# Wide token repeats from a source read four times, and gate rows moved in one piece, in a convolution-attention and expert block

## The reference

```python
t = _to_tokens(x)                       # 4096 tokens per image, 32 features
xn = _ln_t(t)
router_probs = softmax(xn @ router_w + router_b)          # 8 experts
top_p, top_i = top_k(router_probs, 2)
top_p = top_p / sum(top_p)
expert_out = einsum('bnd,edc->bnec', xn, expert_w) + expert_b
t = t + einsum('bnk,bnkc->bnc', top_p, gathered)          # the two best experts, weighted
```

## Time and profile before

| | |
|---|---|
| median of 3 runs | 486.19 us (486.01 to 487.49) |
| profiled execution | 487.85 us, its span 486.2 us |
| busy: PE, DVE, ACT, POOL | 402.4, 390.1, 242.5, 104.6 us |
| DVE, tenths busy in 40 slices of 12.2 us | 0389578999999999999999875976897997997643 |
| DMA share, tenths, same slices | 8400000000000000000000001932164737727541 |
| SP's queue: token repeats, gate moves | 112 of 128 KB, 48 of 32 KB |
| POOL's queue: token repeats, stores | 16 of 128 KB, 16 of 256 KB |

### The profile page before, as it was taken

The page is one execution under the profiler, slowest core; times in us unless marked ns, Lnnn a source line. Parts: engine busy times, 40 slices in busy tenths (PEclk is TensorE's granted clock), DMA queues, the critical chain, the costliest instruction groups (busy, mean ns, idle before and its releaser), DMA issues.

```text
span 486.2 us, 12843 instructions
## 1 busy us (share of the span) xinstructions
PE 402.4 (83%) x4872; PEld 208.5 (43%) x4882; DVE 390.1 (80%) x511; ACT 242.5 (50%) x409; POOL 104.6 (22%) x152
## 2 busy tenths in 40 slices
PE   3786789999999999999999988469688698666863
PEld 1232346666666666666666543124234233111210
DVE  0389578999999999999999875976897997997643
ACT  3653367767777676677767670615323512102110
POOL 6730001011101110110111010003224324524632
PEclk9999779999999999999999998969899989879888
DMA  8400000000000000000000001932164737727541
GB/s 306 184 0 1 2 1 3 1 1 0 0 0 0 0 0 0 0 0 0 0 0 0 3 1 28 205 82 50 38 151 128 167 80 179 187 58 202 140 129 43
DMA packets 10901, 28.80 MB, mean 59 GB/s; under 512 B 3200, under 2 KB 4736, under 8 KB 10496
## 3 DMA queue, kind: packets, MB, share of 16 engines
q1 hardware_dynamic: 8400, 20.46, 16.6%
q0 software_dynamic: 2048, 6.29, 4.3%
q10 hardware_dynamic: 432, 1.77, 0.9%
HBM read 5.96 MB, written 4.19 MB: 21 GB/s over the span
## 4 chain that ended last, share of the span: by engine, by line
PE 45%; DVE 27%; issue 11%; ACT 6%; SPq 5%; DMA 2%; DVEq 1%; POOL 1%; POOLq 0%; ACTq 0%
PE psum L459 7%; DVE neg_max L927 6%; PE psum L321 5%; PE psum L476 5%; PE psum L341 4%; SPq L206 4%; PE psum L446 4%; PE psum L430 4%; DVE window_work L930 3%; PE psum L600 3%; PE psum L484 3%; PE psum L592 3%; PE psum L570 3%; DVE o_tok L938 2%; DVE rstd L363 2%
## 5 line engine op out<-in xcount | busy, mean ns | idle before, releaser
L728 ACT ACTIVATE probs<-psum 128x512 f32<-128x512 f32 x128 | 74.4, 594 | 25.1 <-PE psum L459 24.4
L930 DVE TENSOR_TENSOR window_work<-psum,neg_max 128x1024 f32<-128x1024 f32 x64 | 78.4, 1225 | 7.2
L927 DVE TENSOR_REDUCE neg_max<-psum 128x16 f32<-128x1024 f32 x64 | 77.0, 1203 | 7.3 <-PE psum L446 7.2
L459 PE MATMUL psum<-weights_sb,window_work 128*128 128x128 f32 x512 | 82.1, 283 | 0.9 <-ACT probs L728 0.9
L254 POOL TENSOR_TENSOR o_norm<-o_tok,o_rden 128x128 f32<-128x128 f32 x64 | 24.6, 406 | 249.8 <-DVE o_rden L940 249.8
L459 PEld LDWEIGHTS psum<-weights_sb,window_work 128*128 128x128 f32 x512 | 58.3, 142 | 43.5 <-issue 25.7
L476 PE MATMUL psum<-probs,v_cols 128*32 128x64 f32 x2048 | 55.4, 226 | 0.3 <-DVE o_tok L938 0.3
L592 PE MATMUL psum<-gate_rows,gate_sel_sb 128*128 128x512 bf16 (+1 forms) x118 | 42.3, 407 | 12.8 <-DVE window_work L1075 5.3
L1075 DVE TENSOR_TENSOR window_work<-stage,psum 128x512 f32<-128x512 f32 x48 | 31.8, 676 | 16.3 <-PE psum L592 10.9
L476 PEld LDWEIGHTS psum<-probs,v_cols 128*32 128x32 f32 x2048 | 34.6, 109 | 23.7 <-issue 20.6
L712 ACT ACTIVATE stage<-k_sb,weights_sb 128x512 f32<-128x512 f32 x64 | 44.3, 723 | 0.0
(11 more groups left out here) (95 smaller groups left out, 615.5 us busy)
## 6 DMA issues: line engine op xcount, KB each, us to landing
stage<-x_win SPq DMA_DIRECT2D x112, 128.0 KB, 2.6
out<-out_sb POOLq DMA_DIRECT2D x16, 256.0 KB, 2.5
stage<-in_x SPq DMA_DIRECT2D x3, 1024.0 KB, 14.4
stage<-x_win POOLq DMA_DIRECT2D x16, 128.0 KB, 3.7
gate_rows<-gate_parts SPq DMA_DIRECT2D x48, 32.0 KB, 1.8
stage<-in_x SPq DMA_DIRECT2D x2, 512.0 KB, 6.2
weights_sb<-weights ACTq DMA_DIRECT2D x1, 875.5 KB, 10.3
gate_f<-gate_sel ACTq DMA_DIRECT2D x1, 512.0 KB, 13.5
```

What stands on the lines that cost most here:

```text
L459: last = nc.tensor.transpose(bank[TURN_BANKS[v % 2]][:, b * P:b * P + P], heads.rearrange("p h k -> p (h k)"), const["c_ident"][:, :])
L728: nc.scalar.activation(probs[:, w % 4, :], bank[TURN_BANKS[w % 2]][:, :], ACT.Exp).then_inc(exp_done, 1)
L927: nc.vector.tensor_reduce(m_t, t, AX.X, ALU.max, negate=True).then_inc(max_done, 1)
L930: nc.vector.tensor_tensor(shifted_unit[:, unit % 2, :, :, :], t, m_t.unsqueeze(3).to_broadcast([P, IMG, HEADS, TOK]), ALU.add).then_inc(sh ...
```

## The change

- A token repeat becomes one DMA per image and pair. Its source names each of the 32 channel rows four times (a broadcast dimension behind the partitions), its destination is all 128 partitions of `x_rep`. Row (c, e) now lies in partition 4c + e, where it was 32e + c. All are issued by SP; POOL issues none. Each image has a semaphore of its own, and DVE waits for an image in front of the first unit that uses it.
- A gate move becomes one DMA per chunk: source 32 rows with their three parts, destination 96 rows of `gate_rows`, in the order (row, part). POOL's memset of `gate_rows` goes.
- The weights have to match the new row order. PE regroups the expert weights by a permutation matmul ahead of the attention, DVE builds the permutations (two copies) and copies the result to `experts_sb`. PE selects and reorders the 96 rows of `gate_sel` by two matmuls behind the router of quad 0 (`select_rows`), and ACT writes them as bf16; DVE's cast of `gate_sel` goes.

```diff
             def move_gates(ats):
                 for j, at in enumerate(ats):
-                    for s in range(SPLITS):
-                        sp.dma_start(gate_rows[32 * s:32 * s + 32, bass.ds(at, CHUNK)],
-                                     gate_parts[32 * j:32 * j + 32, s, :]).then_inc(gates_in[j], 16)
+                    sp.dma_start(gate_rows[:, bass.ds(at, CHUNK)],
+                                 gate_parts[32 * j:32 * j + 32, :, :]).then_inc(gates_in[j], 16)
             def repeat_tokens(at, pair):
-                for b in range(IMG if pair == 0 else IMG - POOL_IMAGES):
-                    for e in range(IMG):
-                        sp.dma_start(x_rep[32 * e:32 * e + 32, pair, b, :, :].rearrange("p j n -> p (j n)"),
-                                     t_norm[32 * b:32 * b + 32, bass.ds(at, 2 * CHUNK)]).then_inc(x_rep_in[pair], 16)
+                for b in range(IMG):
+                    sp.dma_start(x_rep[:, pair, b, :, :].rearrange("p j n -> p (j n)"),
+                                 t_norm[32 * b:32 * b + 32, bass.ds(at, 2 * CHUNK)].unsqueeze(1)
+                                 .to_broadcast([C, IMG, 2 * CHUNK])).then_inc(x_rep_in[pair][b], 16)
...
-            pool.memset(gate_rows[:, :], 0.0).then_inc(filled, 1)
...
-                        if j < POOL_IMAGES:
-                            repeat_tokens(i * 2 + u, IMG - 1 - j)
...
+            pe.wait_ge(regroup_ready, 2)
+            nc.tensor.matmul(bank[7][:, 2 * C:4 * C], regroup[:, 0:P],
+                             const["c_we"].rearrange("p a n -> p (a n)"), start=True, stop=True,
+                             skip_group_check=True).then_inc(bias_ps, 1)
...
+            def select_rows(pe):
+                pe.wait_ge(gate_in_loaded, 16)
+                pe.wait_ge(exp_done, CHUNKS * NW + EXP)
+                for u in range(2):
+                    last = nc.tensor.matmul(bank[6 + u][0:SPLITS * 32, :],
+                                            regroup[:, P:P + SPLITS * 32],
+                                            gate_in[:, u * CHUNK:u * CHUNK + CHUNK], start=True, stop=True)
+                last.then_inc(gate_sel_ps, 1)
...
             for j in range(QUAD):
                 router(0, j)
+            select_rows(pe)
             project(CHUNKS - 1, at=5)
...
             gate_logits(0)
+            act.wait_ge(gate_sel_ps, 1)
+            for u in range(2):
+                nc.scalar.activation(gate_sel[:, u * CHUNK:u * CHUNK + CHUNK]
+                                     .rearrange("p (k c e) -> p k e c", k=IMG, c=C),
+                                     bank[6 + u][0:SPLITS * 32, :].rearrange("p (k e c) -> p k e c", k=IMG, e=IMG),
+                                     ACT.Copy).then_inc(gate_sel_ready, 1)
             layer_norm(1)
...
             reciprocals_first(0)
+            dve.wait_ge(weights_loaded, 16)
+            nc.vector.tensor_copy(regroup[:, 0:P].rearrange("p (c e) -> p c e", e=IMG), ...)
+            nc.vector.tensor_copy(regroup[:, P:P + SPLITS * 32].rearrange("p (r s) -> p r s", s=SPLITS), ...)
...
             dve.wait_ge(bias_ps, 1)
+            nc.vector.tensor_copy(experts_sb[:, :, :].rearrange("p a n -> p (a n)"), bank[7][:, 2 * C:4 * C])
...
-            dve.wait_ge(gate_in_loaded, 16)
-            nc.vector.tensor_copy(gate_sel[:, :], gate_in)
...
-                    if j % 2 == 0:
-                        dve.wait_ge(x_rep_in[j // 2], quad * REPEATS[j // 2] + REPEATS[j // 2])
-                    if j == 2:
-                        dve.wait_ge(x_rep_pool, quad * (POOL_IMAGES * IMG * 16) + POOL_IMAGES * IMG * 16)
...
+                            if j % 2 == 0 and k < IMG:
+                                dve.wait_ge(x_rep_in[j // 2][k], quad * 16 + 16)
```

More of the change, by code:

```diff
@@ L89, in metaformer_block @@
         gate_parts = sb("gate_parts", [P, SPLITS, CHUNK], BF16)
-        gate_rows = sb("gate_rows", [P, QUADS * QUAD * CHUNK], BF16)
+        gate_rows = sb("gate_rows", [SPLITS * 32, QUADS * QUAD * CHUNK], BF16)
         logit, logit_t, g_a, g_b, g_mask1, g_mask2, g_rest, gate_t = (
@@ L107, in metaformer_block @@
         gate_in = gate_f32[:, 0:2 * IMG * P]
-        gate_sel = sb("gate_sel_sb", [P, 2 * IMG * P], BF16)
+        gate_sel = sb("gate_sel_sb", [SPLITS * 32, 2 * IMG * P], BF16)
+        experts_sb = sb("experts_sb", [P, 2, C])
+        regroup = sb("regroup", [P, P + SPLITS * 32])
         qb_scaled = sb("qb_scaled", [P, 1])
@@ L136, in metaformer_block @@
         biases_ready = sem("biases_ready")
+        regroup_ready = sem("regroup_ready")
+        gate_sel_ps = sem("gate_sel_ps")
+        gate_sel_ready = sem("gate_sel_ready")
         x_cur_ready = sem("x_cur_ready")
@@ L160, in metaformer_block @@
         gates_in = [sem(f"gates_in{j}") for j in range(QUAD)]
-        x_rep_in = [sem(f"x_rep_in{u}") for u in range(2)]
-        x_rep_pool = sem("x_rep_pool")
+        x_rep_in = [[sem(f"x_rep_in{u}{b}") for b in range(IMG)] for u in range(2)]
         gate_ps = sem("gate_ps")
@@ L175, in metaformer_block @@
         GATE_OPS = 26
-        POOL_IMAGES = 1
-        REPEATS = (IMG * IMG * 16, (IMG - POOL_IMAGES) * IMG * 16)
         DVE_UNITS = 2 * IMG - 2
@@ L212, in _ @@
             repeat_tokens(first[2], 1)
-            sp.wait_ge(filled, 4)
             sp.wait_ge(gate_step, GATE_OPS + ONE)
@@ L268, in scale @@
                 if j % 2 == 0 and i == 0:
-                    pool.wait_ge(x_rep_in[j // 2], quad * REPEATS[j // 2] + REPEATS[j // 2])
+                    pool.wait_ge(x_rep_in[j // 2][0], quad * 16 + 16)
                 pool.wait_ge(gate_copied, c * 2 + (i + 1))
@@ L285, in left @@
                 pool.sem_inc(out_free, 1)
[L287 to L293, removed]
             with pool.Fori(0, QUADS // 2) as i:
@@ L411, in _ @@
             nc.tensor.matmul(bank[7][:, 0:1], const["c_wp"][:, :], const["c_vb"][:, :],
-                             start=True, stop=True).then_inc(bias_ps, 1)
+                             start=True, stop=True)
+            pe.wait_ge(regroup_ready, 2)
+            nc.tensor.matmul(bank[7][:, 2 * C:4 * C], regroup[:, 0:P],
+                             const["c_we"].rearrange("p a n -> p (a n)"), start=True, stop=True,
+                             skip_group_check=True).then_inc(bias_ps, 1)
             def queries(m):
@@ L599, in experts @@
                 for b in range(IMG):
-                    last = nc.tensor.matmul(bank[6 + j % 2][32 * b:32 * b + 32, :], const["c_we"][:, eh, :],
+                    last = nc.tensor.matmul(bank[6 + j % 2][32 * b:32 * b + 32, :], experts_sb[:, eh, :],
                                             scaled[eh * IMG + b], start=False, stop=(eh == 1),
@@ L628, in mixture @@
                 for j in range(QUAD):
-                    pe.wait_ge(gates_in[j], quad * (SPLITS * 16) + SPLITS * 16)
+                    pe.wait_ge(gates_in[j], quad * 16 + 16)
                     for k in range(2 * IMG):
@@ L655, in _ @@
             pe.wait_ge(x2_done, CHUNKS + X2)
+            pe.wait_ge(gate_sel_ready, 2)
             with pe.Fori(0, QUADS - 2) as q:
@@ L807, in gate_copies @@
                     for j in range(QUAD):
-                        act.wait_ge(gates_in[j], quad * (SPLITS * 16))
+                        act.wait_ge(gates_in[j], quad * 16)
                 if step == 21:
@@ L894, in _ @@
             reciprocals_first(0)
+            dve.wait_ge(weights_loaded, 16)
+            nc.vector.tensor_copy(regroup[:, 0:P].rearrange("p (c e) -> p c e", e=IMG),
+                                  const["c_ident"].rearrange("p (e c) -> p c e", e=IMG)).then_inc(regroup_ready, 1)
+            nc.vector.tensor_copy(regroup[:, P:P + SPLITS * 32].rearrange("p (r s) -> p r s", s=SPLITS),
+                                  const["c_ident"][:, 0:SPLITS * 32].rearrange("p (s r) -> p r s", s=SPLITS)
+                                  ).then_inc(regroup_ready, 1)
             with dve.Fori(0, QUADS - 2) as q:
```

## The result

| | before | after |
|---|---|---|
| median us | 486.84 (4 runs) | 505.68 (4 runs, 504.40 to 506.65) |
| ratio after / before | | 1.0384, 95% interval 1.0348 to 1.0420 |
| profiled execution: span us | 486.2 | 504.1 |
| busy: PE, DVE, ACT, POOL | 402.4, 390.1, 242.5, 104.6 | 412.8, 390.9, 245.1, 89.6 |

The change made the kernel 3.8% slower. The forecast was 480.6 with a range of 477.6 to 485.0, so it has the wrong sign.

What follows compares the result with a forecast made beforehand. PE and DVE were both busy, but the order of SP's queue in the last quad was taken to set the end. Terms -7.8 + 0.9 + 0.5 + 1.15 = -5.3 from 486.19 gave 480.9, stated as 480.6, range 477.6 to 485.0.

Steps and rivals of the forecast that it cites:

- the second of "the change part by part": Output stores sharing DMA engines with denser repeats: +0.9 us at the end of quad 1, +0.5 in quad 3.
- The sign of being wrong that came true: Listed as showing the forecast wrong: a new wait of POOL for stores above 2 us.
- Step 1, the queue: SP's queue, quad 3: fewer issues let pair 1 go at its release, DVE's third chunk starting earlier: -7.8 us.
- the gates stand behind pair 0: Quad 3's gate moves queue behind pair 0, first landing near 448.2 us, when PE is free at 448.34: no cost.
- The transfer rate: Token repeats: reads of 32 partitions set the rate, 226 GB/s when full, 9.3 us a pair; chance 0.50.
- Step 3, the regrouping: Gate weights regrouped on PE and ACT before the first mixture, delaying DVE's step 14: +1.15 us, between 0 and 1.7.
- Step 4: Nearly free items: POOL's dropped repeat issues and memset, small DVE copies, a 64-column matmul, the dropped cast: taken as 0.
- The one called slower: Wide repeats under 153 GB/s over a pair make quad 3's tokens and quad 2's gates late: 500 us, chance 0.08.
- Hidden anyway: Row read four times at 150 to 165 GB/s, so quad 3's pairs and gates land late: 485 to 487, chance 0.10.
- The gain goes elsewhere: Queue bad only in the last quad, stores' cost at its upper bound of 4.8 us: 484.3 us, chance 0.10.
- The rival with the fast write side: Writes to 128 partitions set the repeats' rate, 421 GB/s, 5.0 us a pair: 479.7 us, chance 0.22.

Runs made afterwards that it cites:

- The four-buffer version: Changed kernel with four output buffers in place of two, POOL waiting for a store three chunks later: 483.04 us, ratio to before 0.9942.
- the cut in four: Changed kernel with each wide repeat cut into four DMAs by columns (rows of 1 KB, 128 KB each): 484.16 us, ratio to before 0.9959.
- Four buffers beside narrow repeats: Kernel before with wide gate moves, rows of gate_sel selected by PE, and four output buffers; repeats stay narrow: 480.68 us, ratio to before 0.9872.
- The gate half alone: Kernel before with one gate move per chunk, `select_rows` and ACT's two copies; repeats and their rows as before: 482.90 us, ratio to before 0.9934.

## Why the prediction was wrong

**The step that failed** is the second of "the change part by part": "Output stores share the engines with denser repeats", +0.9 and +0.5, "Lower bound of both together 0, upper 2 x (4.9 - 2.5) = 4.8". The overlap was foreseen where it came: at the end of quad 1 the pair starts at 423.12 and the store behind it at 424.58. Its landing was put at 3.4 us, and it took 8.79. The term was off in three ways.

First, the price came from landings beside narrow repeats. These could not show it: SP issued one each 0.59 us and the engines moved one in 0.58, so there can seldom have been many rows ahead of a store; the cut in four, issued as slowly, bears this out with landings of 3.6 us at most. The wide form removes just that limit, and about a dozen rows of 4 KB per engine go before a store's first. Second, I used the maximum of 4.9 us in the earlier trace rows as a bound. That store met repeats that landed in over 4 us, four of them POOL's own in the same queue, so it may have been an early sign. Third, the term was charged at two places where POOL waits at eight.

The four-buffer version takes 22.6 us off. Four buffers beside narrow repeats take 2.2 off (482.90 to 480.68), so about 20 us is what the wide form adds, where 1.4 was taken; in this sum PE's lower clock is included, which the prediction did not have at all. The sign of being wrong that came true was the last one named, a new wait of POOL for stores above 2 us.

**Step 1, the queue.** Right in mechanism. (The issue of a wide repeat was taken at 0.6 us, 2.1 at most; it took 2.3 in the median and up to 3.9.) Its waits in the earlier trace rows are gone, and pair 1 goes at its release. The gate half alone shows a part of the gain: 3 to 4 us less than before. But the -7.8 us is not in the changed kernel: a 10.16 us store now stands in quad 3, ahead of its second chunk, and quad 3 gains 1.3. That the gates stand behind pair 0 was priced at nothing; with four buffers PE waits 5.1 us for them, because a wide pair takes 14.1 us and not 9.3 (next paragraph).

**The transfer rate.** Right in full flow, where reads set it, and wrong for a pair. Windows over the start of a pair's stream and over a full stream of wide repeats in the changed kernel:

```profile
356.00:358.00 2.00, 1.34 (x5) 0.39 (x3) 2.00 (x4) 0.47 (x1) 0.00 (x0) 1.00 0.94 98
...
306.00:310.00 4.00, 2.20 (x8) 0.73 (x12) 3.79 (x7) 3.74 (x8) 0.00 (x0) 1.00 0.93 211
```

211 / 0.93 = 227 GB/s at full share, where 226 was taken and 421 was the rival. The port rule of the Trainium skill (SBUF — State Buffer, Door 1: the DMA port swizzle), read for 32 source partitions, agrees: 218 against 227. Not foreseen is the first 2 us of a pair, at 98 GB/s with busy engines. SP's queue over one wide pair (377.3 to 392 us) and, before, over one narrow pair (355.5 to 368), each with one store beside it:

```profile
q1 hardware_dynamic: 576, 2.10, 75.1%
```

```profile
q1 hardware_dynamic: 769, 2.10, 74.4%
```

The wide pair moves its 2.10 MB from 377.5 to 391.6, which is 14.1 us at 149 GB/s; the narrow one took from 356.3 to 367.9, 11.6 us. The sum had 9.3 and no difference between the two. This is a second term that was too small; what it costs shows where no store is waited for, as PE's 5.1 us for the gates.

**Step 3, the regrouping.** +1.15 taken; the delay came, but nothing is left of it at the first store. PE's two matmuls and ACT's copies in the changed kernel, and the DVE step behind them, against the earlier trace rows:

```profile
301.20 1.88 PE L610 MATMUL psum<-gate_f,regroup 128*96 128x512 f32 x4
...
303.11 2.46 ACT L851 ACTIVATE gate_sel_sb<-psum 96x512 bf16<-96x512 f32 x2 [1.03 <-PE psum L610]
...
313.42 0.20 DVE L1046 TENSOR_SCALAR small<-small 128x64 f32<-128x64 f32 x1 [1.71 <-ACT small L799]
```

ACT's copies took 1.23 us each, not 0.6, and the DVE step waited 1.7 us. It came 15.5 us after the router's start on the chain (297.93), where it was 13.7 before (300.28): 1.8 us later, not 1.1. Yet the first store came 48.8 us after SP's first repeat in both. It was given back before the first mixture: the router's second group of matmuls took 3.60 us after, at a granted clock of 1.00, and 4.22 before, at 0.85. In other profiles the stretch to the first store is 47.7 to 51.9 us, so two profiles can't show a cost of this size, and whether the regrouping costs about a microsecond stays open.

**Step 4.** Nothing in these runs speaks against 0.

**The rivals.** The one called slower gave 500 us and 0.08, for a rate under 153 GB/s over a pair. A wide pair did run at 149. But what this rival built on it, late tokens in quad 3, is in no wait of the changed kernel, and with the same repeats and four buffers the time is 483.0. The sign was right and the mechanism was not. "Hidden anyway" had the rate (150 to 165) and the late gates, and not the stores. "The gain goes elsewhere" named the stores, and bounded them at 484.3. The rival with the fast write side has two totals, 479.5 in the sum and 479.7 in the list; its terms give 479.7, and nothing hangs on the difference.

## What to carry to other kernels

When a stream of DMAs is bound by its issues, that limit also keeps little ahead of the transfers of other queues. Before merging many DMAs into few, look for a transfer that an engine waits for, and price it behind a full queue and not by its landings so far. If it can't be kept away from the stream, give it buffers so that no one waits for it (two more buffers of 256 KB gave back 22.6 us), or keep the rows of the stream short (2 KB rows in place of 4 gave back 19).

## What the runs showed that was not expected

- What goes ahead of another queue's transfer is a number, not an amount of bytes: with 4 KB and with 2 KB rows 10 to 16 packets per engine went ahead of a store's first, in 5 to 6 us and in 2 to 3. Whether it counts rows or DMAs is open.
- A wide repeat alone runs at 148 GB/s at full share, several in full flow at 227, and a whole pair at 149 on average. Why was not tried and stays open.
- Executions of one and the same stage come in two kinds. From 44 to 60 us PE's mean granted clock is 0.79 or 1.00; windows of before and after:

```profile
44.00:60.00 16.00, 10.34 (x47) 4.41 (x45) 11.03 (x23) 5.82 (x9) 0.00 (x0) 0.79 0.01 2
```

```profile
44.00:60.00 16.00, 9.60 (x80) 4.02 (x78) 13.16 (x26) 6.74 (x11) 0.00 (x0) 1.00 0.01 2
```

The expert stage starts 2.4 us later with the first kind (301.04 and 298.68 us). It is not tied to the edit: the four-buffer version, which has the same code up to there as the changed kernel, shows 0.79 and 301.24. Over the 14 profiles here, five have 0.79 and start the stage at 301.04 to 301.51, nine have 1.00 and start it at 298.44 to 299.22. Two single profiles can differ by this much, which is why the loss above is counted from the stage's own start.
